# A two-layer graph network kernel on one core: the matrix engine takes two pairs of source tiles per step, and one buffer holds what three held

## The reference, cut to what matters

```python
def _L1_gnn_ref(H, A, W, a_l, a_r):
    mask = A + jnp.eye(n, dtype=A.dtype) > 0
    Wh = (H @ W).reshape(n, N_HEADS, D_K)
    sl = jnp.einsum('nhd,hd->nh', Wh, a_l)
    sr = jnp.einsum('nhd,hd->nh', Wh, a_r)
    e = jax.nn.leaky_relu(sl[:, :, None] + sr.T[None, :, :], negative_slope=NEG_SLOPE)
    e = jnp.where(mask[:, None, :], e, -jnp.inf)
    alpha = jnp.nan_to_num(jax.nn.softmax(e, axis=2), nan=0.0)
    out = jnp.einsum('nhm,mhd->nhd', alpha, Wh).reshape(n, OUT_DIM)
    return jax.nn.elu(out)
```

## Time and profile before

| what | us |
|---|---|
| median of 3 runs | 894.61 (885.39 to 895.58) |
| the profiled execution, device time | 890.09 |
| its span, first to last instruction | 888.4 |
| PE busy in the span | 820.1 (92%) |
| DVE busy | 720.9 (81%) |
| ACT busy | 696.0 (78%) |
| GpSimd busy | 154.5 (17%) |
| layer 1's first product | at 400.47 |

### The profile page before, as it was taken

One profiled execution on the slowest core, in us unless ns is written; L12 is line 12 of the kernel. 1 busy time (PEld: TensorE's weight loads), 2 busy tenths in 40 slices (PEclk: granted clock), 3 DMA queues, 4 the chain that ended last, 5 costly groups with the idle time before them and its releaser, 6 DMA issues.

```text
span 888.4 us, 26591 instructions
## 1 busy us (share of the span) xinstructions
PE 820.1 (92%) x10273; PEld 656.4 (74%) x10273; DVE 720.9 (81%) x1367; ACT 696.0 (78%) x987; POOL 154.5 (17%) x221
## 2 busy tenths in 40 slices
PE   3998899999999999719999989999899999899996
PEld 3444455555555555309999989999899999899996
DVE  3897687878787877549889898888998889989885
ACT  2676566666666666259999998999999999989993
POOL 0111354546464645100000000000000000000000
PEclk9999999999999999959999999999999999999999
DMA  7346777787878788250041011041101410111011
GB/s 218 101 156 217 277 262 297 286 311 285 315 283 321 277 315 245 51 127 3 24 94 48 0 47 48 10 84 48 47 0 47 95 48 0 47 48 48 0 24 35
DMA packets 74873, 115.30 MB, mean 130 GB/s; under 512 B 55552, under 2 KB 57472, under 8 KB 66656
## 3 DMA queue, kind: packets, MB, share of 16 engines
q1 hardware_dynamic: 63344, 93.14, 31.9%
q0 software_dynamic: 7376, 20.85, 7.4%
q10 hardware_dynamic: 4128, 1.05, 0.6%
HBM read 98.17 MB, written 16.85 MB: 129 GB/s over the span
## 4 chain that ended last, share of the span: by engine, by line
PE 49%; DVE 5%; issue 1%; ACT 1%; DMA 0%; DVEq 0%; ACTq 0%
PE acc L936 49%; DVE sgn L1075 2%; DVE pos L1083 1%; DVE sgn L1065 1%; DVE val L1109 1%; DMA srow<-s_scratch 0%; ACT sgn L986 0%; DVE vtmp L1101 0%; DVE total L1116 0%; DVE yout L1147 0%; DVE ey L1142 0%; DVE total L1121 0%; DVE yout L1134 0%; ACT val L996 0%; ACT ey L1009 0%
## 5 line engine op out<-in xcount | busy, mean ns | idle before, releaser
L986 ACT ACTIVATE sgn<-srow,rbias 128x1024 int8<-128x1024 f32 x384 | 404.7, 1167 | 3.5 <-DMA srow<-s_scratch 2.5
L936 PE MATMUL acc<-val,sgn 128*128 128x130 f16 x4096 | 257.0, 220 | 22.1 <-DVE val L1109 14.7
L936 PEld LDWEIGHTS acc<-val,sgn 128*128 128x128 fp8e4 x4096 | 240.7, 97 | 23.3 <-issue 22.8
L936 PE MATMUL acc<-val,pos 128*128 128x130 f16 x4096 | 253.8, 219 | 2.0 <-DVE pos L1083 2.0
L936 PEld LDWEIGHTS acc<-val,pos 128*128 128x128 fp8e4 x4096 | 238.3, 97 | 2.4 <-issue 2.4
L430 PE MATMUL ps_a<-g,mT 128*128 128x512 f16 x1024 | 236.2, 385 | 2.5 <-DVE mT L696 2.5
L1075 DVE SCALAR_TENSOR_TENSOR sgn<-sgn,mask 128x1024 int32<-128x1024 int32 x128 | 156.4, 1222 | 44.5 <-ACT sgn L986 43.9
L430 PEld LDWEIGHTS ps_a<-g,mT 128*128 128x128 fp8e4 x1024 | 101.4, 99 | 113.5 <-issue 9.1
L533 ACT ACTIVATE junk<-bits 128x2048 uint8<-128x2048 uint8 x64 | 122.2, 1910 | 68.2 <-DVE bits L685 63.4
L1065 DVE TENSOR_SCALAR sgn<-srow,rbias 128x1024 uint8<-128x1024 f32 x128 | 96.0, 750 | 3.0 <-DMA srow<-s_scratch 3.0
L1083 DVE TENSOR_SCALAR pos<-sgn 128x1024 int32<-128x1024 int32 x128 | 87.9, 687 | 9.1 <-PE acc L936 9.1
(11 more groups left out here) (104 smaller groups left out, 613.8 us busy)
## 6 DMA issues: line engine op xcount, KB each, us to landing
stage<-in_adj SPq DMA_DIRECT2D x64, 1024.0 KB, 6.1
srow<-s_scratch SPq DMA_DIRECT2D x16, 512.0 KB, 4.5
mask<-in_x SPq DMA_DIRECT2D x16, 256.0 KB, 2.7
own_scratch<-mask POOLq DMA_DIRECT2D x16, 256.0 KB, 3.0
xt<-in_x POOLq DMA_DIRECT2D x32, 128.0 KB, 3.0
own<-own_scratch POOLq DMA_DIRECT2D x32, 128.0 KB, 5.5
x_scratch<-x POOLq DMA_DIRECT2D x32, 128.0 KB, 2.1
x1s<-x_scratch SPq DMA_DIRECT2D x16, 256.0 KB, 3.4
```

Of the source, the lines that this page charges most:

```text
L936: last = nc.tensor.matmul(acc[j][:, br * VBLK:(br + 1) * VBLK], bytes_of(ring[:, k % size, j * (P // 2):(j + 1) * (P // 2)])[:, b, :], val ...
L986: nc.scalar.activation(sign_bytes(sgn, k, b), srow[:, gr % 2, :], ACT.Sign, bias=rbias[:, 0, gr // NS, 2 * k + b:2 * k + b + 1]).then_inc( ...
```

## The change

PE's unit becomes the chunk: it waits for z of both pairs, does 64 negative products (8 per bank), raises the new `pe_neg`, waits for pos of both pairs and does 64 positive ones. `pe_pair` is raised once per chunk instead of once per pair. The ring `pos` has eight slots (four pairs) instead of four. The slots of `sgn` are awaited through `wait_neg`: the negative products of the chunk must be through, and the positive bytes of the pair made. The quotient and the exponential lose their own buffers: `y` is now the first 64 columns of `total`, `ey` columns 65 to 128. So `read_minus`, which overwrites `total`, waits until the last store has landed, and `divide` no longer does.

```diff
-PR = 4
+PR = 8
...
-        y = sb("yout", [P, NJ, DK], F32)
-        ey = sb("ey", [P, NJ, DK], F32)
+        y = total[:, :, 0:DK]
+        ey = total[:, :, DV:DV + DK]
...
         def wait_pair(eng, gr, q):
...
-            if q < NQ - 1:
-                eng.wait_ge(pe_pair, gr * (NQ - 1) + q + 1)
+            if q < NQ - 2:
+                eng.wait_ge(pe_pair, gr * (NCH - 1) + q // 2 + 1)
             else:
                 eng.wait_ge(pe_bank, (gr + 1) * NJ)
+
+        def wait_neg(eng, gr, q):
+
+            if gr * NQ + q >= 0:
+                eng.wait_ge(pe_neg, (gr * NQ + q) // 2 + 1)
+                eng.wait_ge(pos_ready, gr * NQ + q + 1)
...
-                                 y[:, :, :].rearrange("p (k e) d -> p e k d", e=2)[:, e]).then_inc(stored, 16)
+                                 total[:, e:NJ:2, 0:DK]).then_inc(stored, 16)
...
             with pe.Fori(0, NG) as gr:
-                for q in range(NQ):
-                    if 2 * q % CH == 0:
-
-                        pe.wait_ge(val_ready, gr // NS * (NCH * 2) + (2 * q // CH + 1) * 2)
-
-                    pe.wait_ge(z_ready, gr * NQ + (q + 1))
+                for c in range(NCH):
+
+                    pe.wait_ge(val_ready, gr // NS * (NCH * 2) + (c + 1) * 2)
+
+                    pe.wait_ge(z_ready, gr * NQ + (2 * c + 2))
                     hold(pe, waits_passed)
                     for j in range(NJ):
-                        if q == 0:
+                        if c == 0:
 
                             pe.wait_ge(plus_ready, gr * NJ + (j + 1))
                             hold(pe, waits_passed)
-                        branch(q, j, 1, z32, ZR)
-
-                    pe.wait_ge(pos_ready, gr * NQ + (q + 1))
+                        last = branch(c, j, 1, z32, ZR)
+
+                    last.then_inc(pe_neg, 1)
+                    pe.wait_ge(pos_ready, gr * NQ + (2 * c + 2))
                     hold(pe, waits_passed)
                     for j in range(NJ):
-                        last = branch(q, j, 0, pos, PR)
-                        if q == NQ - 1:
+                        last = branch(c, j, 0, pos, PR)
+                        if c == NCH - 1:
                             last.then_inc(pe_bank, 1)
-                    if q < NQ - 1:
+                    if c < NCH - 1:
                         last.then_inc(pe_pair, 1)
...
-                wait_pair(act, gr, q - ZR // 2)
+                wait_neg(act, gr, q - ZR // 2)
...
                     if j == 0 and gr:
-                        act.wait_ge(div_ready, gr)
+                        act.wait_ge(stored, gr * 32)
...
-                wait_pair(dve, gr, q - ZR // 2)
+                wait_neg(dve, gr, q - ZR // 2)
...
                 dve.wait_ge(den_step, gr * 2 + 2)
-                if gr:
-                    dve.wait_ge(stored, gr * 32)
```

More of the change, by code:

```diff
@@ L845, in layer1 @@
         pe_pair = sem("pe_pair")
+        pe_neg = sem("pe_neg")
         pe_bank = sem("pe_bank")
@@ L930, in bytes_of, with branch @@
                 return t.bitcast(F8).rearrange("p (n b) -> p b n", b=2)
-            def branch(q, j, br, ring, size):
-                for k in (2 * q, 2 * q + 1):
+            def branch(c, j, br, ring, size):
+                for k in range(CH * c, CH * (c + 1)):
                     for b in range(2):
@@ L1008, in exps @@
                 act.wait_ge(div_ready, gr + 1)
-                nc.scalar.activation(ey[:, :, :], y[:, :, :], ACT.Exp).then_inc(exp_ready, 1)
+                nc.scalar.activation(ey, y, ACT.Exp).then_inc(exp_ready, 1)
             for gr in range(NG):
@@ L1131, in divide @@
                 dve.wait_ge(den_step, gr * 2 + 2)
-                if gr:
-                    dve.wait_ge(stored, gr * 32)
-                nc.vector.tensor_tensor(y[:, :, :], total[:, :, 0:DK],
+                nc.vector.tensor_tensor(y, total[:, :, 0:DK],
                                         den[:, 1, :].unsqueeze(2).to_broadcast([P, NJ, DK]), ALU.mult
@@ L1141, in add_x1 @@
                 dve.wait_ge(x1_in, (gr + 1) * 16)
-                nc.vector.scalar_tensor_tensor(ey[:, :, :], ey[:, :, :], 1.0, x1s[:, :, :], ALU.min, ALU.add
+                nc.vector.scalar_tensor_tensor(ey, ey, 1.0, x1s[:, :, :], ALU.min, ALU.add
                                                ).then_inc(add_step, 1)
@@ L1146, in finish @@
                 dve.wait_ge(add_step, gr + 1)
-                nc.vector.scalar_tensor_tensor(y[:, :, :], y[:, :, :], 0.0, ey[:, :, :], ALU.max, ALU.add
+                nc.vector.scalar_tensor_tensor(y, y, 0.0, ey, ALU.max, ALU.add
                                                ).then_inc(y_ready, 1)
```

## The result

The changed kernel takes 904.79 us (median of 8 runs, 900.71 to 906.46) where the kernel before took 893.37 (8 runs, 885.39 to 895.58). The ratio is 1.013, interval 1.010 to 1.015: slower, by 11.4 us in the medians, and less than 2%. The forecast was 905, and +13.1 on like executions.

What follows compares the result with a forecast made beforehand. PE was taken to bound ordinary groups, sixteen runs of 1.82 us. Terms 9.3 + 2.9 + 1.1 - 0.2 = +13.1 us gave 903.2 on the profiled execution; forecast 905, 8-in-10 range 892 to 913.

Steps and rivals of the forecast that it cites:

- nine such groups: Ordinary groups 1, 2, 5, 6, 9, 10, 13, 14 and 15: PE waits 1.03 us in each, 9.3 us together.
- three head changes against before: Head changes: PE waits on DVE's results; +1.5 and +1.4 us for two, 0 for the first, together 2.9.
- start of layer 1: PE's step 3 is wanted at 416.5 us, but z of pair 5 reaches it at 417.6: +1.1 us.
- end: End of the kernel: reads trail PE's last product by 0.19 us less, so -0.2 us.
- The supply of signs: After ACT's bank reads: z of pair 3 reaches PE at T+8.31, wanted T+7.28, so PE waits 1.03 us a group.
- the ring: Larger pos ring: DVE could start pos earlier, but is late by its own work; 0 us.
- the strided rows: Strided y and ey in sums and the division: 0, at most 0.1 us of DVE, hidden by its spare time.
- the store wait: ACT's wait for the last store before read_minus: cost 0, with 2.3 us of cover.
- the 11.5 us of the far end: Halving PE's waits could save at most 11.5 us if the spacing excess were all theirs; taken as zero.
- The rival that the deeper ring would free DVE: Head changes: eight slots and released reads remove PE's waits, -12.7 us, giving 879, or 867 at the far end; chance 0.05.
- The clock: Rival: PE's waits in every group bring 1.2 GHz stretches; 928, or 911 if in one of four; chance 0.07.

Runs made afterwards that it cites:

- the run with one sign ahead: Changed kernel with the first of ACT's three signs of pair 2 issued before the eight bank reads instead of after; 893.42 us, ratio 1.000.
- the fourth sign on ACT: DVE's fourth sign of pair 2 made by ACT in every group: on the changed kernel 918.40 us, on the kernel before 893.00 us.
- the half change: Kernel before with y and ey inside total and eight slots of pos, but still a step of one pair; 893.78 us, ratio 1.001.
- the later products: Making of val for the next head spread later: kernel before 889.99 us, the half change 888.07, changed kernel with one sign ahead 888.32.
- the products on GpSimd: DVE's products for the next head moved to GpSimd: kernel before 893.51 us, changed kernel 908.29, changed kernel with one sign ahead 898.52.

## Why the prediction was right

The sum, step by step, with lengths from the starts of PE's runs; T is the start of a group.

| step | forecast | measured |
|---|---|---|
| first sign after the reads | T+0.45 | T+0.47 |
| second step starts, ordinary group | T+8.31 | T+8.24 |
| wait there | 1.03 | 0.96 |
| period of an ordinary group | 30.13 | 30.04 |
| nine such groups | +9.3 | +8.4 |
| head change: start of step 4's negative run | T+23.42 | T+23.34 |
| its positive run | T+27.92 | T+27.89 |
| next group | T+32.38 | T+32.35 |
| its first positive run | T+37.44 | T+37.41 |
| its second step | T+41.58 | T+41.51 |
| length of groups 7 and 8 | 63.38 | 63.32 |
| three head changes against before | +2.9 | +2.7 |
| start of layer 1 | +1.1 | +1.0 |
| end | -0.2 | -0.2 |
| sum | +13.1 | +11.9 |

The profiled spans differ by 10.7, because layer 1's first product came 1.2 us earlier in the one after (399.28 against 400.47), and nothing of the change lies ahead of it.

**The supply of signs.** It is the mechanism, shown from both sides: one sign less in the chain takes the loss away (the run with one sign ahead), one more adds 1.04 us a group to the wait (the fourth sign on ACT), and the same sign with the step of one pair adds 0.1 us to the group. The term was 0.07 us too large for each group: from the first sign to z of pair 3 it is 6.44 us instead of 6.49, from z to PE 0.10 instead of 0.15, and 0.02 went the other way. Why was not tested. The prediction counts the 6.44 as six signs of ACT's; DVE's own work is as long in the second half of it; that changes no number of the sum.

**What was put at zero.** The step as such, the ring, the strided rows and the store wait are zero within what these runs can tell: by the half change (ratio 1.001, 0.997 to 1.005, groups of 29.10 us) and by the run with one sign ahead, which has all of them (1.000, groups of 29.08). The stores of the changed kernel landed as before, and no wait of ACT names one:

```profile
DMA to landing us min/median/max: 2.0/2.1/2.3
```

That PE's waits as such cost nothing was right too: runs of 64 start 3.62 to 3.65 us apart, twice 1.82, so the 11.5 us of the far end were not there.

**The head changes.** DVE's gapless run kept its times, as the table shows. The rival that the deeper ring would free DVE falls: with the ring and the old step the waits are 0.82 and 2.65 us, as without. The experiments behind it refine this. The waits are due to DVE's work, but not to its sum alone: ACT's signs up to pair 1 come next, and with the later products ACT's and DVE's rows both fill a head's first group, which takes 30.8 us. Each removal brought only a part, and my forecasts of what would come next were too good by 5 to 13 us, but for one.

**The clock.** After the first head change the changed kernel kept its full clock, as assumed. That rival gets no support from ordinary groups: they have a mean clock of 1.00 with a wait of 0.96 us in each, and with the fourth sign on ACT still 1.00 with 2.00 us in each.

**The number.** 905 against 904.79 is closer than the working deserves: a sum 1.2 too large, and a base, the mean of four executions at 891.4, 2.0 below the median of eight at 893.4. The two errors go against each other, and that part of the agreement is luck.

## What to carry to other kernels

When a consumer's step is made coarser, look for the producer that starts anew from the consumer's own last product, and count from there. As long as its order stays, no buffer depth helps such a chain; that follows from the order of the program, and of the two rings only the one for positive bytes was deepened in a run. Here the chain had 2.4 us to spare, the coarser step asks for its result 3.6 us earlier, and the engines' busy shares told nothing of it. Where a producer waits for a release and has other work that is allowed already, put just so much of it ahead of the wait as fits into the wait; and when one wait goes, work out the next before counting the gain.

## What was not expected of the hardware

- GpSimd's multiplication holds up DVE: tensor_scalar operations of 0.75 and 0.69 us took 1.55 and 1.54 us beside it, and GpSimd's own took 1.05 to 2.5 us. It was seen at each of the three head changes of that run.
- Granted clock after long waits of PE: the kernel before ran a stretch at 1.2 GHz behind its first head change (waits 0.82 and 2.65 us), and the half change, with the same waits, behind its third. Such a stretch costs 1.5 us. With the products on GpSimd it came behind two of three, with one sign ahead as well behind all three, and in the changed kernel with them, after waits just as long, behind one. The changed kernel, with waits of at most 1.42 us, had none in layer 1's head changes. Each kernel has one profiled execution, so whether the kernel or chance decides which is hit isn't known.
- Layer 0 carries most of the spread between executions: in 14 profiled ones, with the same code for it, layer 1's first product comes at 396.0 to 405.7 us, while an ordinary group repeats to 0.03 us within either kernel. A comparison of layer 1 is better made from that start.
